# A two-layer gated cross-attention kernel: half of a normalised x transposed inside the attention's drain, and the operations of the middle in another order

## The chip, the cores and the metric

The kernel runs on one core of a Trainium2 chip. The metric is the time of one execution on the device in microseconds (us). TensorE (PE) multiplies and transposes, VectorE (DVE) and ScalarE (ACT) work element by element and empty the PSUM banks that TensorE fills, GpSimd (POOL) works element by element in SBUF and issues the indirect DMAs, and SyncE (SP) issues the plain DMAs. Each engine takes its instructions in the order in which they are written, and they wait for each other by semaphores (`wait_ge`).

## The reference, cut to what matters

x is 8 blocks of 128 tokens by 512 features, and the context has the same shape. Four residual updates follow each other:

```
x = x + tanh(g_xattn[0]) * cross_attention(layernorm(x), ctx)      # 32 heads, 8 kv heads
x = x + tanh(g_ffn[0])   * permuted_ffn(layernorm(x))              # t[:, perm], 16 small ffns, gelu, t[:, unperm]
x = x + tanh(g_xattn[1]) * group_attention(layernorm(x), ctx, ctx)
x = x + tanh(g_ffn[1])   * experts(layernorm(x))                   # top-1 of 8 experts
```

The third one is what the middle of the kernel computes (q is the normalised x, k and v are the context):

```
t = Wt @ v;  p = Wp @ q;  g = Wg @ k                 # products over the 128 tokens of a block
att = sum over a group of (p * g)                    # 8 groups of 16 tokens
y = Wz @ (att * t), group by group                   # so y = att * z with z = (Wz Wt) @ v
yn = (y - mean(y)) * rsqrt(var(y) + eps), in a group # var(y) = att^2 * var(z)
out = yn * gn_w + gn_b + v                           # v is the context, the residual
```

## The kernel before, in words

**Attention.** 64 units (8 groups g of heads, 8 blocks b) run through a software pipeline. For each engine the function `run` is given a list of stages, each with the number of units that it runs ahead or behind, and calls them in the list's order in every step. A unit goes through the q projection (L835 to L837), the scores (L825), mask and maximum (L750, L753), exponentials (L576), the transposition of p (L852), the values (L876 to L878), and the output projection (L865 to L867), of which `accumulate` (L782) adds the result to x. The last steps, in which no q projection is left, are the drain. Some stages do something only there, when `after(u, b, g, last)` holds: four of eight z products (`z01`, `z2`, `z3`, L893, one product of 512 columns each, copied to `s.z` by ScalarE, L652), and the first half (blocks 0 to 3) of the second layer norm: seed, Newton step on GpSimd, normalisation (L712, L811), transposition on TensorE into four PSUM banks (`transpose_x`, L888), and copies to `s.xT2` (`copy_xT`, L646, L803). `transpose_x` stands in the list with an offset of -5, behind the last unit's values, and the z products 2 and 3 ahead of it. They use banks 0 and 1, as the transpositions of blocks 0 and 1 do.

**Feed-forward.** In `middle`, SyncE stores the transposed x in four pieces of two blocks (L998, 512 KB each). Ahead of the first it waits for the last output projection (L562). GpSimd gathers the permuted features back in four indirect DMAs for each half (L1113), TensorE multiplies by `up` (L1289), ScalarE applies gelu (L1061), and TensorE multiplies by `down` (L1299). This goes in 12 packs: four of 512 tokens for the first half, eight of 256 for the second. VectorE copies the results (L1176), GpSimd scatters them (L1094: four for blocks 0 to 3, four for 4 and 5, four for 6 and 7), and SyncE loads each third (L1002), which TensorE transposes back (`transpose_y`, L1249) and VectorE adds to x (L1184).

**Middle.** For each third of the blocks: statistics of x on VectorE (L101, L104), half the variance plus eps (`layernorm_var`, L117), a seed for rsqrt by logarithm and exponential on ScalarE (`seed3`, L1038, L1040), a Newton step on GpSimd (`rstd3`, four small operations, L75 to L81), the shift -mean*rstd on VectorE (`negated_shift`, L110), the normalisation on ScalarE (`normalise3`, L1046), the product with Wp (`p_product`, L1258), and the product with g summed along the row on VectorE (L1216). GpSimd scales the context (`scale_ctx`, L1088) and adds it to x in place (`add_ctx`, L1108), which waits until ScalarE has normalised the block. ScalarE centres z (L1078), eight operations, ahead of the seed for y's variance (L1080, L1082). Then comes a Newton step on GpSimd and `a_col` on VectorE (L1234).

**Experts.** VectorE forms x3 = z * a_col + x block by block (`update`, L1506) with its statistics (L1511), TensorE transposes it (`transpose_x3`, L1667), the gate (L1673), logits (L1680), ranks and tile list follow, GpSimd scatters the rows to their experts (L1480), and 15 tiles of 128 rows go through the chosen experts' weights (L1744 to L1751).

The order around the change is written out by hand, in the lists of `run` and in the code of `middle` and `experts`.

## Time and profile before

| | us |
|---|---|
| median of 3 runs | 802.3 |
| lowest, highest | 801.92, 802.57 |
| profiled execution | 801.22 |
| its span | 799.4 |
| TensorE busy in the span | 748.2 |
| ScalarE, VectorE, GpSimd busy | 484.5, 469.5, 310.4 |

The mean granted clock of TensorE is 0.974 of full speed. The profiled execution's own time is longer than its span, since the span runs from the first to the last instruction. A share of busy time is a mean over stages: from 160 to 560 us TensorE is busy in every slice, and in the last fifth of the span its share falls to 0.6 to 0.9 in places. The lines L.. are those of the kernel before. "Idle before <-" names what ended the idle time of an engine.

### The profile page before, as it was taken

The page shows a single profiled execution, that of the slowest core. Times are in us where ns is not written, and L with a number is a line of the kernel's source. Part 1 is how long each engine was busy: PE and PEld are TensorE (multiplying, and loading weights), DVE is VectorE, ACT ScalarE, POOL GpSimd, SP SyncE. Part 2 cuts the span into 40 slices and gives each one's busy share as a digit, 9 for nine tenths or more (in the row PEclk, how much of TensorE's full clock was granted, in tenths as well). Part 3 has the DMA queues.
Part 4 walks back from the last instruction along what each step waited for, and adds up shares of the span by engine and source line. Part 5 has one row for each costly group of instructions (what it writes and reads, how often), then busy time and mean ns, then how long its engine had stood idle before and what let it go on. Part 6 is the DMA issues. An engine that isn't in the chain of part 4 may idle for free.

```text
span 799.4 us, 13560 instructions
## 1 busy us (share of the span) xinstructions
PE 748.2 (94%) x3925; PEld 604.0 (76%) x3925; DVE 469.5 (59%) x891; ACT 484.5 (61%) x1817; POOL 310.4 (39%) x623
## 2 busy tenths in 40 slices
PE   5999987999999999999999999999999979767997
PEld 3788876888888887888888788888887633336775
DVE  4786404565656565656565556565657645887652
ACT  4543336767676766676767566667665547456831
POOL 0331015353443453444354335354422336624242
PEclk9999999999999999999999999999999989966999
DMA  8545451302303303032132230330430065834232
GB/s 302 178 133 172 131 188 67 120 24 110 134 14 120 127 21 119 17 115 82 62 119 74 71 119 13 118 132 13 129 105 2 1 192 182 325 144 141 88 106 79
DMA packets 42125, 87.76 MB, mean 110 GB/s; under 512 B 5561, under 2 KB 26041, under 8 KB 38226
## 3 DMA queue, kind: packets, MB, share of 16 engines
q1 hardware_dynamic: 38884, 78.71, 29.1%
q0 software_dynamic: 3184, 8.41, 3.0%
q8 instruction: 21, 0.34, 0.2%
q14 instruction: 36, 0.29, 0.1%
HBM read 70.28 MB, written 35.57 MB: 132 GB/s over the span
## 4 chain that ended last, share of the span: by engine, by line
PE 71%; DVE 5%; ACT 4%; issue 2%; DMA 1%; POOL 1%; POOLq 0%; ACTq 0%; SPq 0%; DVEq 0%
PE banks L865 7%; PE banks L867 7%; PE banks L866 7%; PE banks L837 7%; PE banks L835 7%; PE banks L836 7%; PE banks L825 6%; PE banks L844 4%; PE banks L852 3%; PE banks L1750 2%; PE banks L1751 2%; PE banks L1749 2%; PE banks L876 2%; PE banks L878 2%; PE banks L877 2%
## 5 line engine op out<-in xcount | busy, mean ns | idle before, releaser
L576 ACT ACTIVATE p_sb<-p_sb,nmax 128x128 f32<-128x128 f32 x256 | 99.8, 391 | 132.2 <-DVE nmax L753 132.2
L674 POOL TENSOR_TENSOR v_lo<-v_raw,v_hi 128x128 fp32r<-128x128 f32 x64 | 29.6, 462 | 255.1 <-ACT v_hi L614 255.1
L776 DVE TENSOR_TENSOR pT_lo<-banks,pT_hi 128x512 fp32r<-128x512 f32 x64 | 44.2, 691 | 49.8 <-ACT pT_hi L589 49.8
L825 PEld LDWEIGHTS banks<-kT,qT_sb 128*128 128x128 f32 x512 | 67.0, 192 | 6.7 <-ACT qT_sb L584 1.8
L825 PE MATMUL banks<-kT,qT_sb 128*128 128x128 f32 x512 | 67.9, 276 | 1.4 <-ACT qT_sb L584 1.4
L679 POOL TENSOR_TENSOR p_sb<-p_sb,rsum 128x512 f32<-128x512 f32 x64 | 66.6, 1041 | 5.5 <-DVE rsum L772 5.5
L621 ACT ACTIVATE q_junk<-banks 128x128 f32<-128x128 f32 x256 | 66.1, 273 | 1.8 <-PE banks L837 1.8
L744 DVE TENSOR_TENSOR oT_lo<-banks,oT_hi 128x512 fp32r<-128x512 f32 x64 | 44.1, 689 | 35.6 <-ACT oT_hi L571 35.5
L398 PE MATMUL banks<-w_hi,ctx_hi 128*128 128x512 f32 x128 | 53.6, 419 | 9.3 <-DVE ctx_lo L329 9.3
L782 DVE SCALAR_TENSOR_TENSOR x_sb<-banks,tgates,x_sb 128x512 f32<-128x512 f32 x64 | 48.1, 751 | 15.2 <-PE banks L867 13.7
L571 ACT ACTIVATE oT_hi<-banks 128x512 fp32r<-128x512 f32 x64 | 38.0, 594 | 31.2 <-PE banks L878 27.0
L760 DVE TENSOR_SCALAR q_val<-q_ss 128x4 f32<-128x4 f32 x64 | 31.9, 498 | 41.3 <-ACT q_junk L621 41.3
L772 DVE RECIPROCAL rsum<-prob_sum 128x4 f32<-128x4 f32 x64 | 11.4, 178 | 72.2 <-ACT p_sb L576 72.2
L835 PE MATMUL banks<-w_hi,xT_hi 128*128 128x512 f32 x128 | 53.2, 416 | 0.0
L865 PE MATMUL banks<-odd_hi,oT_hi 128*128 128x512 f32 x128 | 52.9, 414 | 0.3 <-DVE oT_lo L744 0.2
L621 ACT ACTIVATION_READ_ACCUMULATOR q_junk<-banks 128x1 f32 x256 | 53.0, 207 | 0.0
L865 PE MATMUL banks<-w_hi,oT_hi 128*128 128x512 f32 x128 | 52.8, 412 | 0.0
L835 PE MATMUL banks<-odd_hi,xT_hi 128*128 128x512 f32 x128 | 52.6, 411 | 0.0
L400 PE MATMUL banks<-w_lo,ctx_hi 128*128 128x512 f32 x128 | 51.0, 398 | 0.0
L399 PE MATMUL banks<-w_hi,ctx_lo 128*128 128x512 f32 x128 | 50.7, 396 | 0.0
L837 PE MATMUL banks<-w_lo,xT_hi 128*128 128x512 f32 x128 | 50.6, 395 | 0.0
L836 PE MATMUL banks<-w_hi,xT_lo 128*128 128x512 f32 x128 | 50.5, 394 | 0.0
(271 smaller groups left out, 2099.7 us busy)
## 6 DMA issues: line engine op xcount, KB each, us to landing
sorted_x<-in_empty SPq DMA_DIRECT2D x8, 2064.0 KB, 9.1
w_raw<-in_wq_l SPq DMA_DIRECT2D x8, 1024.0 KB, 5.3
w_raw<-in_wo_l SPq DMA_DIRECT2D x8, 1024.0 KB, 4.8
exp_w<-in_exp_w_l SPq DMA_DIRECT2D x8, 1024.0 KB, 8.4
kT_scr<-kT_st SPq DMA_DIRECT2D x16, 256.0 KB, 2.3
v_scr<-v_st SPq DMA_DIRECT2D x16, 256.0 KB, 2.3
xs<-sorted_x SPq DMA_DIRECT2D x15, 258.0 KB, 2.8
v_raw<-v_scr SPq DMA_DIRECT2D x14, 256.0 KB, 2.6
```

Of the source, the lines that this page charges most:

```text
L398: pe.matmul(kv_ps[i % 3][:, :], ctx_hi[:, kt, tok], hi, start=(kt == 0), stop=False)
L400: last = pe.matmul(kv_ps[i % 3][:, :], ctx_hi[:, kt, tok], lo, start=False, stop=(kt == KT - 1))
L576: last = act.activation(p_sb[:, b % 2, h * P:(h + 1) * P], p_sb[:, b % 2, h * P:(h + 1) * P], ACT.Exp, bias=nmax[:, b % 2, h:h + 1], accum ...
L621: last = act.activation(junk[:, h * P:(h + 1) * P], q_ps[b % 2][:, h * P:(h + 1) * P], ACT.Square, accum_out=ss[:, b % 2, h:h + 1])
L679: pool.tensor_tensor(blocks(p_sb[:, b % 2, :]), blocks(p_sb[:, b % 2, :]), per_block(rsum[:, b % 2, :], P), ALU.mult).then_inc(p_done, 1)
L825: last = pe.matmul(s_ps[:, h * P:(h + 1) * P], qT_sb[:, b % 2, h * P:(h + 1) * P], kT[:, b * P:(b + 1) * P], start=True, stop=True)
L835: pe.matmul(q_ps[b % 2][:, :], xh, wq_hi[odd][:, kt, :], start=(kt == 0), stop=False)
L836: pe.matmul(q_ps[b % 2][:, :], xl, wq_hi[odd][:, kt, :], start=False, stop=False)
L837: last = pe.matmul(q_ps[b % 2][:, :], xh, wq_lo[odd][:, kt, :], start=False, stop=(kt == KT - 1))
L865: pe.matmul(o_ps[b % 2][:, :], oh, wo_hi[odd][:, h, :], start=(h == 0), stop=False)
L866: pe.matmul(o_ps[b % 2][:, :], ol, wo_hi[odd][:, h, :], start=False, stop=False)
L867: last = pe.matmul(o_ps[b % 2][:, :], oh, wo_lo[odd][:, h, :], start=False, stop=(h == HG - 1))
```

## The change

It has these parts:

- In the drain, `transpose_x` moves from behind the last values to ahead of the values of unit 62. The normalisation on VectorE moves ahead of `p_recip`. ScalarE copies three of four blocks, VectorE one. The z products 2 and 3 move behind the transpositions and wait for the copies of banks 0 and 1. The copies of z 2 and 3 stand at ScalarE's end. SyncE's wait for the last output projection is left out, and the stores wait for the copies by the new counts.
- GpSimd scales the context between its gathers and first scatters. `add_ctx` writes into the scaled context's own tile, so it no longer waits for the normalisation; x3 is formed from that tile, and the transposed x3 moves to where x was.
- The shift of the third layer norm is computed on GpSimd from a negated mean. The seeds read the variance itself. The first product of p and g stands ahead of the updates of blocks 6 and 7. ScalarE centres z in three groups. The variance of y is computed by a shorter way, its Newton step on VectorE.
- In the experts part, TensorE multiplies 128 columns of g by the unit matrix, nine times ahead of x3's first transposition and twice after each. Nothing reads the results: they go to a bank that the logits overwrite later.

```diff
             sp.dma_start(s.ctx_nat[:, :, :], d.ctx).then_inc(s.ctx_nat_ld, 16)
-            sp.wait_ge(o_done, UNITS)
...
-            run(act, [(oT_split, -2), (exps, 0), (copy_z01, 0), (qT_copy, 1), (pT_split, -1), (copy_z2, -1), (copy_z3, -1),
-                      (v_split, 2), (q_stats, 2), (seed_ln2, -3), (copy_xT, -6), (split_bias, 0)]
+            run(act, [(oT_split, -2), (exps, 0), (copy_z01, 0), (qT_copy, 1), (pT_split, -1), (copy_xT, -4), (copy_z23, -2),
+                      (v_split, 2), (q_stats, 2), (seed_ln2, -3), (split_bias, 0)]
...
-            run(dve, [(oT_split, -2), (mask_max, 0), (q_scale, 1), (p_recip, 0), (pT_split, -1), (q_half, 2),
-                      (copy_xT, -6), (normalise_ln2, -5), (accumulate, -2), (x_stats, -2), (split_bias, 0)])
+            run(dve, [(oT_split, -2), (mask_max, 0), (normalise_ln2, -4), (q_scale, 1), (p_recip, 0), (pT_split, -1), (q_half, 2),
+                      (accumulate, -2), (copy_xT, -4), (x_stats, -2), (split_bias, 0)])
...
             def z2(u, b, g, odd):
-                if after(u, b, g, B - 2):
-                    pe.wait_ge(s.z_copied[1], 1)
+                if after(u, b, g, B - 1):
+                    pe.wait_ge(xT_copied[1], 1)
                     z_product(2)
 
             def z3(u, b, g, odd):
                 if after(u, b, g, B - 1):
-                    pe.wait_ge(q_scaled, UNITS)
+                    pe.wait_ge(xT_copied[1], 2)
                     z_product(3)
...
-            run(pe, [(scores, 0), (q_proj, 2), (z01, 0), (q_transpose, 1), (p_transpose, -1), (z3, -1), (o_proj, -2),
-                     (z2, -1), (values, -1), (transpose_x, -5)])
+            run(pe, [(scores, 0), (q_proj, 2), (z01, 0), (q_transpose, 1), (p_transpose, -1), (z2, -1), (o_proj, -2),
+                     (transpose_x, -4), (values, -1), (z3, -1)])
...
                     if c == 0:
-                        sp.wait_ge(xT_copied[1 - pair], 2)
+                        sp.wait_ge(xT_copied[1], 2 + pair)
+                        reached(sp, xT_copied[0], pair)
...
             def seed3(c):
                 cols = slice(*THIRDS[c])
-                act.wait_ge(xval3_done, c + 1)
-                act.activation(xtmp[:, cols], xval[:, cols], ACT.Ln, scale=2.0).then_inc(xln3_ln, 1)
+                act.wait_ge(mv_done, THIRDS[c][1])
+                reached(act, xrstd3_done, c)
+                act.activation(xln3[:, cols], mv[:, cols, 1], ACT.Ln, bias=s.eps[:, 0:1]).then_inc(xln3_ln, 1)
...
             seed3(0)
             copy_g(5)
             copy_g(6)
             normalise3(0)
+            seed3(1)
+            centre(0, 1)
+            normalise3(1)
             copy_g(7)
-            seed3(1)
-            normalise3(1)
             seed3(2)
+            centre(2)
             normalise3(2)
-            act.wait_ge(col_step, 3)
-            for b in range(B):
-
-                act.activation(s.z[:, b, :], s.z[:, b, :], ACT.Identity, bias=s.nmean[:, b:b + 1]).then_inc(centred, 1)
-            act.wait_ge(yval_done, 1)
-            act.activation(yln[:, :], yval[:, :], ACT.Ln, scale=2.0).then_inc(yln_done, 1)
+            centre(3, 4, 5, 6, 7)
+            act.wait_ge(att_step, 2)
+            act.activation(yln[:, :], yvar[:, :], ACT.Ln, bias=s.eps[:, 0:1]).then_inc(yln_done, 1)
...
+                pool.wait_ge(xrstd3_done, c + 1)
+                pool.wait_ge(negm_done, c + 1)
+                pool.tensor_tensor(xshift[:, cols], negm[:, cols], xrstd[:, cols], ALU.mult).then_inc(xshift3_done, 1)
+
+            def add_ctx(*bs):
                 for b in bs:
                     pool.wait_ge(ctx_scaled, b + 1)
-                    pool.wait_ge(xln3_done, b + 1)
-                    pool.tensor_tensor(s.x[:, b, :], s.x[:, b, :], ctx_res[:, b, :], ALU.add).then_inc(res_done, 1)
+                    pool.wait_ge(x_done, b + 1)
+                    pool.tensor_tensor(ctx_res[:, b, :], s.x[:, b, :], ctx_res[:, b, :], ALU.add).then_inc(res_done, 1)
...
             def update_x(b):
-                if b == HB:
-                    shift(0)
                 dve.wait_ge(y_done, b + 1)
...
             updates_with_stats(dve, s, update_x, x_done, bn_done, mv_done, xval3_done, THIRDS[1:2])
+            negate_mean(1)
+            product(0)
             updates_with_stats(dve, s, update_x, x_done, bn_done, mv_done, xval3_done, THIRDS[2:3])
-            shift(1)
...
                 last.then_inc(x3T_done, 1)
+                keep_warm(2)
+
+            def keep_warm(n):
+                for i in range(n):
+                    pe.matmul(logit_ps[1][:, 0:P], s.ident[:, :], s.g[:, 0, 0:P], start=True, stop=True)
...
             pe.wait_ge(s.row_done, B)
+            keep_warm(9)
             for b in range(HB):
                 transpose_x3(b)
...
-            s.x3T = [beside(f"x3T{c}", [P, KT, HALF], 8 * c) for c in range(2)]
+            s.x3T = [s.at(f"x3T{c}", [P, KT, HALF], 8 * c) for c in range(2)]

```

TensorE in the drain, before: from the end of output projection 61, with z product 2 (L893), the values of unit 62 (L876 to L878), p's last transposition (L852) and z product 3.

```order
L893 MATMUL banks<-ctx_nat,mT 128x512 [waits z_copied1]
L876 MATMUL banks<-pT_hi,v_hi 128x512 [waits xT1_hi_done,kvw_lo_done,xrstd1_done]
L877 MATMUL banks<-pT_hi,v_lo 128x512
L878 MATMUL banks<-pT_lo,v_hi 128x512
L852 MATMUL banks<-ident_sb,p_sb 128x128 [waits xrstd1_done,xval1_done]
L852 MATMUL banks<-ident_sb,p_sb 128x128 x3
L893 MATMUL banks<-ctx_nat,mT 128x512 [waits kv_free]
```

The same place in the changed kernel, from its third transposition of x on (`hid` is the normalised x, L884 the transpositions, L871 the values, L847 p's, L889 the z product). Semaphores can bear the name of an earlier owner.

```order
L884 MATMUL banks<-ident_sb,hid 128x128 [waits xln2_done1]
L884 MATMUL banks<-ident_sb,hid 128x128 x3
L871 MATMUL banks<-pT_hi,v_hi 128x512 [waits xT1_hi_done,kvw_lo_done,xrstd1_done]
L872 MATMUL banks<-pT_hi,v_lo 128x512
L873 MATMUL banks<-pT_lo,v_hi 128x512
L847 MATMUL banks<-ident_sb,p_sb 128x128 [waits xrstd1_done,xval1_done]
L847 MATMUL banks<-ident_sb,p_sb 128x128 x3
L889 MATMUL banks<-ctx_nat,mT 128x512 [waits xT2_copied1]
```

The 16 transpositions of x took z product 2's place; z product 2 took z product 3's; and z product 3 went behind the last values, where the transpositions were.

GpSimd in the middle, before: from the last eight scatters (L1094) to its first additions.

```order
L1094 DMA yT_scr<-xg,perm_col 512x256 [waits yT_copied] x8
L1088 TENSOR_SCALAR ctx_res<-ctx_nat,tgates,tb 128x512 x2
L75 TENSOR_TENSOR xtmp<-xseed 128x4 [waits xseed3_done]
L77 TENSOR_TENSOR xtmp<-xtmp,xval 128x4 [waits newton3]
L79 TENSOR_TENSOR xtmp<-three_halves,xtmp 128x4 [waits newton3]
L81 TENSOR_TENSOR xrstd<-xseed,xtmp 128x4 [waits newton3]
L1088 TENSOR_SCALAR ctx_res<-ctx_nat,tgates,tb 128x512 x4
L1108 TENSOR_TENSOR x_sb<-x_sb,ctx_res 128x512 [waits xln3_done,ctx_scaled] x2
```

The same stretch in the changed kernel.

```order
L1098 DMA yT_scr<-xg,perm_col 512x256 [waits yT_copied] x8
L1116 TENSOR_TENSOR ctx_res<-x_sb,ctx_res 128x512 [waits x2_done,ctx_scaled] x2
L75 TENSOR_TENSOR xtmp<-xseed 128x4 [waits xval3_done,xseed3_done]
L77 TENSOR_TENSOR xtmp<-xtmp,xval 128x4 [waits newton3]
L79 TENSOR_TENSOR xtmp<-three_halves,xtmp 128x4 [waits newton3]
L81 TENSOR_TENSOR xrstd<-xseed,xtmp 128x4 [waits newton3]
L1110 TENSOR_TENSOR xshift<-neg_mean,xrstd 128x4 [waits neg_mean3_done,xrstd3_done]
L1116 TENSOR_TENSOR ctx_res<-x_sb,ctx_res 128x512 [waits x2_done,ctx_scaled] x2
```

The scalings are gone from here: two now stand between the two halves' gathers, and the other six between those gathers and the scatters of the first third. Additions stand ahead of each Newton step, and the shift behind it.

## Rows read from the trace of the kernel before

**Rows 1.** Chain of waits, 641 to 656 us: start us, us, what
```profile
642.52 0.39 SPq L998
...
642.96 4.07 DMA xT_scr<-xT
...
647.31 1.19 POOL xg L1113
```

**Rows 2.** Timeline, TensorE, drain to y's transpositions: start us, us, instruction [idle before <-releaser]
```profile
630.18 1.02 PE L893 MATMUL banks<-ctx_nat,mT 128*128 128x512 f32 x2
631.52 0.50 PE L876 MATMUL banks<-pT_hi,v_hi 128*128 128x512 f32 x1 [0.33 <-DVE pT_lo L776]
...
637.45 1.91 PE L888 MATMUL banks<-ident_sb,hid 128*128 128x128 f32 x16
639.29 0.50 PE L865 MATMUL banks<-odd_hi,oT_hi 128*128 128x512 f32 x1
...
652.26 1.62 PE L1289 MATMUL banks<-xg,up 32*128 32x512 f32 x8 [4.06 <-DMA xg<-xT_scr,perm_col]
...
663.60 0.71 PE L1289 MATMUL banks<-xg,up 32*128 32x256 f32 x8
...
677.92 2.17 PE L1249 MATMUL banks<-ident_sb,xT 128*128 128x128 f32 x16
```

**Rows 3.** Windows of 5 us: busy us of each engine, granted clock, DMA share, GB/s
```profile
655.00:660.00 5.00, 5.00 (x24) 1.19 (x20) 1.03 (x2) 2.77 (x3) 3.06 (x4) 0.54 0.66 175
710.00:715.00 5.00, 4.11 (x32) 2.68 (x31) 4.96 (x13) 3.27 (x7) 1.15 (x4) 0.92 0.00 0
715.00:720.00 5.00, 3.68 (x21) 1.69 (x19) 4.19 (x17) 1.63 (x5) 0.00 (x0) 0.76 0.00 0
```

**Rows 4.** Timeline, ScalarE, the middle
```profile
699.74 5.00 ACT L1078 ACTIVATE z<-z,nmean 128x512 f32<-128x512 f32 x8
704.64 0.19 ACT L1080 ACTIVATE yln<-yval 128x8 f32<-128x8 f32 x1
```

**Rows 5.** Timeline, VectorE, small operations of the middle
```profile
644.77 0.16 DVE L75 TENSOR_TENSOR xtmp<-xseed 128x4 f32<-128x4 f32 x1 [0.38 <-ACT xseed L1020]
...
688.91 1.32 DVE L117 TENSOR_SCALAR xval<-mv 128x2 f32<-128x2 f32 x1
...
697.08 1.20 DVE L110 SCALAR_TENSOR_TENSOR xshift<-mv,xrstd 128x2 f32<-128x2 f32 x1 [1.79 <-POOL xrstd L81]
...
706.22 0.17 DVE L1234 TENSOR_TENSOR a_col<-att,yrstd 128x8 f32<-128x8 f32 x1 [2.29 <-POOL yrstd L81]
```

**Rows 6.** Timeline, TensorE, the gate's products
```profile
711.96 1.07 PE L1673 MATMUL banks<-x3T,gate_c 128*32 128x512 f32 x8 [0.69 <-ACT x3T L1421]
...
717.39 1.74 PE L1673 MATMUL banks<-x3T,gate_c 128*32 128x512 f32 x8 [0.69 <-ACT x3T L1421]
```

**Rows 7.** Chain of waits, a unit of attention
```profile
584.96 0.89 PE banks L825 x8
```

**Rows 8.** Timeline, GpSimd, drain to the middle
```profile
625.60 4.15 POOL L712 TENSOR_SCALAR hid<-x_sb,mv,xrstd 128x512 f32<-128x512 f32 x2
...
654.28 0.94 POOL L1113 DMA_INDIRECT xg<-xT_scr,perm_col  x1 [2.02 <-DMA xT_scr<-xT]
...
668.14 1.52 POOL L1088 TENSOR_SCALAR ctx_res<-ctx_nat,tgates,tb 128x512 f32<-128x512 f32 x2
...
678.80 0.97 POOL L1094 DMA_INDIRECT yT_scr<-xg,perm_col  x1 [0.30 <-issue]
...
688.93 2.51 POOL L1108 TENSOR_TENSOR x_sb<-x_sb,ctx_res 128x512 f32<-128x512 f32 x2
```

**Rows 9.** DMA issues, 625 to 745 us: out<-in, queue, count, KB each, median us to landing
```profile
xT<-yT_scr SPq DMA_DIRECT2D x1, 1024.0 KB, 5.5
...
yT_scr<-xg,perm_col POOLq DMA_INDIRECT x12, 2.7
```

**Rows 10.** DMA issues, 654 to 659.5 us, the second half's gathers
```profile
xg<-xT_scr,perm_col POOLq DMA_INDIRECT x4, 3.9
```

116 lines of the change are left out of this document (64 added, 52 removed).

## The prediction

> **What bounds the kernel now.** I read the chain of waits first, then TensorE's timeline from the last attention units on, then the windows, and GpSimd's, ScalarE's and VectorE's timelines beside them. Up to 620 us TensorE is full and the change leaves its order alone there. From 642 us nothing is full: the chain goes through a store, a gather, chains of small operations, and TensorE runs partly at half clock. The whole change lies in 620 to 730 us, so the sum is made on that stretch; the tiles of the experts behind it (a full TensorE) only shift. The profiled execution took 801.22 us, span 799.4 and 1.8 around it; the median shown is 802.3, 1.1 above it.
>
> Four things fix the length of the stretch. (1) The store of the first half of xT, 4.07 us, starts at 642.96, after the last output projection, and the first gather of GpSimd follows it; TensorE stands still for 4.06 us until 652.26 [rows 1, 2]. (2) Its clock is then at 0.54 of full on average from 655 to 660, that is 1.2 GHz for nearly all of it [rows 3]. (3) In the middle, the coefficient a_col is ready at 706.22 + 0.17 = 706.39, behind eight centrings of z on ScalarE (5.00 us), a logarithm at 704.64, and a Newton step on GpSimd for which VectorE waits 2.29 us [rows 4, 5]. (4) From there to the tiles VectorE and TensorE alternate, and TensorE's clock comes and goes: the gate's eight instructions take 1.07 us at 711.96 and 1.74 at 717.39 [rows 6].
>
> **Drain of the attention.** After output projection 61, TensorE had z product 2 (from 630.18) and a wait, and came to unit 62's values at 631.52. Now the 16 transpositions, 1.91 us with the tail of the last (1.84 from start to start, 639.29 less 637.45), stand there: values at 632.0, 0.5 late [rows 2]. The other end: the second normalisation of GpSimd (4.15 us for two, ended at 629.75 [rows 8]) and VectorE's two, now ahead of its reciprocal, may collide, which I bound at one more of GpSimd's, 2.1 us late. Behind them wait values, the last transposition of p and the projection. Later the 16 transpositions are gone from 637.45, and a z product (0.9, from 1.02 us for one with its tail) stands there instead. Yet the last projection starts when VectorE has split oT, 639.29 before, and VectorE's row is the same there: I take 0.3 late, between 0 and 2. The three copies of xT on ScalarE, under 0.6 us each like its centrings, stand ahead of unit 62's oT and end by 632.5, before those values are done at 632.9. **Term A: +0.3.**
>
> A second cost stands at 644.7. GpSimd now scales two blocks of the context (0.76 each [rows 8]) just when VectorE runs its Newton step at 644.77 [rows 5]. In these rows a small VectorE operation takes 1.32 us (a tensor_scalar of 128x2) or 1.20 (a product of two SBUF inputs) while GpSimd adds blocks, against 0.16 for the Newton step's without it [rows 5]. So one or two of the five small operations can stand behind a block: 0 to 1.5 us, I take 0.4, as the blocks are short. **Term B: +0.4.** The Trainium skill, SBUF — State Buffer, § Who interferes with whom, has the rule: the port pair that VectorE and GpSimd share is a lock, so the later one waits for the whole instruction of the other; two SBUF inputs or a two-port mode take it. The two rows agree. By it this change, which puts GpSimd's blocks beside VectorE's statistics, has a price of its own: it is the last rival below.
>
> **Feed-forward.** SyncE no longer waits for the last projection: the first pair of blocks is stored at about 632.3 and the second at 633, landed by 637.5 with 4.07 us a store [rows 1]; four gathers, 1.25 us apart and landed 3.9 us after their start [rows 10], are done by 646. TensorE then starts the first pack as soon as the second half's copies are done. They ended at 648.8 on ScalarE and 649.4 on VectorE, so it starts at 649.7 instead of 652.26: 2.55 us. Its idle time shrinks from 4.06 to under 1.5, so I take the full clock for the first packs. Pack 4 started 11.3 us after pack 0, 663.60 less 652.26 [rows 2]. At full clock a pack of 512 columns takes 2.4 to 2.5 us, by which pack 4 comes 8.8 us after pack 0 with the first gelu waiting for the table load: 2.5 us. **Term C: −5.1** (−2.6 if the clock drops all the same, or if the second half's gathers, at 654.28 [rows 8], stay where they are: these must land by 658.5, 3.9 us from their start [rows 10], and start at 653 to 653.7 now that the second store has the transfers to itself).
>
> GpSimd gives some of that back. Its order is now: gathers until 658.0; two scalings 1.5; four times a scatter (0.97 and 0.3 between) and a scaling 0.76, the fourth scatter starting at 665.6; landed 2.7 later; load of yU 5.5: 673.9 [rows 8, 9]. Before, the transpositions of y started at 677.92 [rows 2]. So TensorE waits for that load and not for the feed-forward (which ends at 671): I gain 3.9, not 5.1. The eight scatters behind end at 678.4, were 679.77, and the last load, half as large, lands by 684.2, for a transposition due at 684.9: no wait. **Term D: +1.2** (0 to +3).
>
> **Middle, from y to a_col.** Per step:
> - The shift for x3's normalisation moves from VectorE to GpSimd. For VectorE it was a wait before block 4, and 1.20 us behind an addition for the last group. One small operation, 0.2 us as GpSimd's others, and a hand-over replace it; the seed reads the variance itself, so the half variance (1.32 us beside GpSimd's additions [rows 5]) leaves ScalarE's chain.
> - ScalarE's order becomes seed 1, centre 0 and 1, normalise, seed 2, centre 2, normalise, centre 3 to 7. Three centrings (1.9 us) now lie in waits for GpSimd. The last normalisation ended just ahead of the centrings at 699.74 [rows 4]; by the new order, reckoned with the 3.9, it ends at 693.4.
> - Five centrings (5 x 0.62) end at 696.5, when the variance of y is ready too (last product 695.3, sum over groups 0.6, two small operations). Logarithm and exponential 0.45, Newton on VectorE four times 0.2, a_col 0.2: 698.0.
> Against 706.39 that is 8.35, of which 3.9 are counted: **Term E: −4.4** (−2.5 to −6). The additions of the context, 1.25 us each [rows 8], lose their wait for the normalisation, and end by 694.4, ahead of the 698.
>
> **Unread products.** Nine stand after the sum over groups, two after each of eight transpositions, 25 in all, 128 columns each: 0.22 us at full clock (0.89 for eight instructions, four products), some 0.45 at half [rows 7]. The first nine take 2.0 to 4.0 us in TensorE's wait for a_col and x3, which is about 3 now; a pair and a transposition take 0.9 (1.7 cold) against VectorE's 1.27 a block, so they hold nothing up once the clock is full. Before, the clock was back at full for most of 710 to 715 (mean 0.92), behind x3's first transpositions, and lower again in 715 to 720 (0.76) [rows 3]. Kept full through the ranks and logits (the gate 0.67 less [rows 6], the logits and two groups of rank products, each of a like length, some 0.6 to 0.9), both the tile list and the scatters would come 2 us sooner: the second comes through GpSimd's scatters, which follow each other. The products stop at the last transposition, though, so I take part: **Term F: −1.4** (+0.9, if cold products delay x3, to −2.2). The Trainium skill, TensorE: Matmul & The Clock Gate, § What's actually happening, says the throttled clock is the default and activity releases it, with which the rise at 710 agrees.
>
> Sum: 0.3 + 0.4 − 5.1 + 1.2 − 4.4 − 1.4 = −9.0. So 801.22 − 9.0 = 792.2 for a profiled execution, and 802.3 − 9.0 = **793.3** as the median.
>
> **Rivals.**
> - *More passes through.* GpSimd's queue is not the bound (loads land sooner, D = 0), the clock holds to the tiles (F = −2.2), B = 0: −11.4, 790.9. For it: the landings are medians of few [rows 9]. Against: twelve scatters at 1.27 apart are a fixed queue. Chance 0.2.
> - *The early store is hidden.* The second half's gathers or GpSimd's longer queue bound the feed-forward, so C and D together give 1.0 and not 3.9: −6.1, 796.2. For it: pack 4 needs the gather from the second store, whose start moves only by 1. Against: the gathers that started at 654.28 had landed 5 us ahead of pack 4 at 663.60. Chance 0.2.
> - *Unread products are in the way.* The clock is at half when they start and x3's transpositions fall behind VectorE: F = +0.9 instead of −1.4, and 0.7 of E lost: −6.0, 796.3. Chance 0.07.
> - *Slower: VectorE stands behind GpSimd.* Seven operations at 644 to 646 (Newton, shift, two normalisations) behind a scaling of 0.76, and ten in the middle (three half variances, three negated means, four on the deviations of z) behind an addition of 1.25: 5.3 + 12.5 = 17.8 us if each waits a whole one. With 0.4 already counted: −9.0 + 17.4 = +8.4, 810.7. It decides from about half of them (9.4 us) on. For it: 1.32 and 1.20 [rows 5]. Against: GpSimd's blocks fill only parts of that time, and the half variance is no longer what ScalarE waits for. Chance 0.04. This is what the rule of the page SBUF — State Buffer in the Trainium skill, § Who interferes with whom, would do here.
>
> My forecast has 0.49. What this measurement can tell from no change is 0.2%, 1.6 us. All cases but the last and a corner of the two partial ones are faster: 0.93, same 0.02, slower 0.05. Range: from 789.5 (the first rival with E at −5.8) to 797.2 (the partial ones with A at 1.3), leaving out the slow one and the tails.
>
> **What would show it.** SyncE's first store near 632 and the first gather near 637.5; TensorE's first up product near 650 with a granted clock of 1.00 behind it; y's transpositions near 674 behind a load; a_col near 698; a clock of 1.00 from there to the last x3 transposition; the tiles starting near 731. It would be wrong if pack 4 or the y transpositions don't move, if small VectorE operations of over 1 us stand ahead of xrstd or a_col, or if the last projection is over 2 us late.

## The result, and the profile after

The changed kernel took 796.38 us (median of four executions, 795.69 to 799.69); the kernel before took 802.11 us in the same comparison. The ratio is 0.9946, 95% interval 0.9929 to 0.9964: 0.5% faster, where 1.1% was forecast. The sign and the range were right. The size was not: by the ratio half of the forecast gain was missing, by the medians (5.7 us gained of 9.0) a good third. Timed again beside the experiments, the changed kernel took 796.18 us (six executions, 794.83 to 799.52), ratio 0.9935, interval 0.9914 to 0.9956. Ratios here and below leave out three slow executions: one of 1089 us of the kernel before, and one each (865 and 856 us) of two of the later kernels.

There are two profiles of it. The first fell on the slowest of its four executions (799.69 us). The second (span 793.5 us, clock 0.988) is nearer to the median, and the rows below are from it where nothing else is said. This table cuts the spans at the same points of the program, in us:

| from one point to the next | before | changed, first profile | changed, second profile |
|---|---|---|---|
| start to the eight z products | 642.16 | 642.51 | 641.89 |
| to the first pack of the feed-forward | 10.10 | 7.54 | 7.55 |
| to the first g products (feed-forward done) | 23.84 | 21.25 | 21.24 |
| to y's first transpositions | 1.82 | 5.96 | 4.90 |
| to y's transpositions of blocks 4, 5 | 6.66 | 10.73 | 8.08 |
| to the first p product | 3.28 | 3.29 | 3.28 |
| to the end of a_col | 18.53 | 13.72 | 13.72 |
| to the split of the experts' weights (ew_lo) | 23.39 | 22.22 | 22.21 |
| to the first tile | 12.34 | 12.95 | 12.34 |
| to the end of the span | 57.28 | 57.63 | 58.29 |

In the fourteen profiles of this study the z products started between 640.3 and 644.4, though the code ahead of them is of two kinds only: where an execution stands at that point says little of the edit. So positions are counted from there. From the end of output projection 61 to the z products, however, the drain takes the same time in every execution of one order: 11.96 to 12.00 us in the three profiles with the drain of before (642.16 less 630.18 is 11.98), 12.38 to 12.40 in the eleven with the changed drain (641.89 less 629.50 is 12.39).

TensorE's timeline answers to [rows 2, 6]. The 16 transpositions stand at 629.50, ahead of the values. The first pack comes 7.55 behind the z products, and the fifth (658.17) 8.73 us after it, not 11.34. Behind the g products the engine has nothing for 2.91 us, and then y's 16 transpositions take 3.32 us instead of 2.17. The gate's two groups take 1.06 and 1.07 us (1.07 and 1.74 before).

```profile
629.50 1.91 PE L884 MATMUL banks<-ident_sb,hid 128*128 128x128 f32 x16
631.16 0.48 PE L871 MATMUL banks<-pT_hi,v_hi 128*128 128x512 f32 x1
...
641.89 3.59 PE L1251 MATMUL banks<-ctx_nat,mT 128*128 128x512 f32 x8
...
649.44 1.99 PE L1304 MATMUL banks<-xg,up 32*128 32x512 f32 x12 [0.73 <-DVE xT L1158]
...
658.17 0.71 PE L1304 MATMUL banks<-xg,up 32*128 32x256 f32 x8
...
670.68 1.98 PE L1255 MATMUL banks<-ctx_nat,wgT 128*128 128x512 f32 x4
675.58 3.32 PE L1261 MATMUL banks<-ident_sb,xT 128*128 128x128 f32 x16 [2.91 <-DMA xT<-yT_scr]
...
706.08 1.06 PE L1694 MATMUL banks<-x3T,gate_c 128*32 128x512 f32 x8 [0.24 <-ACT x3T L1436]
...
711.91 1.07 PE L1694 MATMUL banks<-x3T,gate_c 128*32 128x512 f32 x8 [0.24 <-ACT x3T L1436]
```

The windows answer to [rows 3], in the same columns. 655 to 660 is at 1.00 where it was 0.54; the new hole is in 675 to 680; 710 to 715 is at 1.00 where it was 0.92.

```profile
655.00:660.00 5.00, 4.79 (x40) 1.20 (x33) 3.34 (x8) 4.83 (x6) 4.05 (x6) 1.00 0.55 152
675.00:680.00 5.00, 4.42 (x26) 4.45 (x26) 3.52 (x7) 0.00 (x0) 3.98 (x5) 0.66 0.56 194
710.00:715.00 5.00, 4.06 (x35) 2.94 (x33) 4.22 (x20) 2.57 (x6) 0.60 (x3) 1.00 0.01 3
```

GpSimd's timeline [rows 8]: gathers of the first half from 636.09, the two scalings that stand beside VectorE's Newton step, the second half's gathers, two more scalings, the fourth scatter. The load of yU can be issued only when this has landed.

```profile
636.09 1.19 POOL L1125 DMA_INDIRECT xg<-xT_scr,perm_col  x1 [5.21 <-DMA xT_scr<-xT]
...
644.30 1.52 POOL L1092 TENSOR_SCALAR ctx_res<-ctx_nat,tgates,tb 128x512 f32<-128x512 f32 x2 [3.26 <-DVE tb L1167]
654.46 0.98 POOL L1125 DMA_INDIRECT xg<-xT_scr,perm_col  x1 [8.63 <-DMA xT_scr<-xT]
...
659.23 1.51 POOL L1092 TENSOR_SCALAR ctx_res<-ctx_nat,tgates,tb 128x512 f32<-128x512 f32 x2
...
666.93 1.03 POOL L1098 DMA_INDIRECT yT_scr<-xg,perm_col  x1 [0.17 <-issue]
```

VectorE, then ScalarE [rows 4, 5]: two of four Newton operations take 0.58 and 0.48 us where they took 0.16, the half variance is down from 1.32 to 0.73, a_col no longer waits for GpSimd, and five centrings are left ahead of the logarithm.

```profile
644.50 0.58 DVE L75 TENSOR_TENSOR xtmp<-xseed 128x4 f32<-128x4 f32 x1 [0.38 <-ACT xseed L1019]
...
645.36 0.48 DVE L79 TENSOR_TENSOR xtmp<-three_halves,xtmp 128x4 f32<-128x4 f32 x1
...
687.15 0.73 DVE L117 TENSOR_SCALAR xval<-mv 128x2 f32<-128x2 f32 x1
...
700.49 0.17 DVE L1246 TENSOR_TENSOR a_col<-att,yrstd 128x8 f32<-128x8 f32 x1
```

```profile
696.06 3.15 ACT L1067 ACTIVATE z<-z,nmean 128x512 f32<-128x512 f32 x5
699.13 0.28 ACT L1084 ACTIVATE yln<-yvar,eps 128x8 f32<-128x8 f32 x1
```

The first profile shows the same wait in a worse execution: here the fourth scatter needed 4.14 us to land and the load of yU 5.38 (chain of waits), and TensorE came back from 3.98 idle us at half clock for longer.

```profile
667.59 4.14 DMA yT_scr<-xg,perm_col
...
671.75 5.38 DMA xT<-yT_scr
```

```profile
677.26 3.65 PE L1261 MATMUL banks<-ident_sb,xT 128*128 128x128 f32 x16 [3.98 <-DMA xT<-yT_scr]
```

### The profile page after: what moved, and what is told of

Read it like the earlier page. It is cut to its first block, busy times and chain, and to the rows that moved or that the text cites. A ratio compares the mean times of both kernels' runs of the same rounds, so it can differ in the third digit from the quotient of the medians.

```text
span 797.8 us, 13672 instructions
## 1 busy us (share of the span) xinstructions
PE 751.3 (94%) x3975; PEld 610.2 (76%) x3975; DVE 468.2 (59%) x893; ACT 485.4 (61%) x1818; POOL 310.7 (39%) x622
## 4 chain that ended last, share of the span: by engine, by line
PE 70%; DVE 6%; ACT 4%; issue 2%; DMA 1%; POOL 1%; POOLq 0%; ACTq 0%; DVEq 0%
PE banks L860 7%; PE banks L862 7%; PE banks L861 7%; PE banks L832 7%; PE banks L831 7%; PE banks L830 7%; PE banks L820 6%; PE banks L839 4%; PE banks L847 3%; PE banks L1771 2%; PE banks L1772 2%; PE banks L1773 2%; PE banks L873 2%; PE banks L871 2%; PE banks L872 2%
```

## The experiments

My theory after the two profiles was this: the early store gives what was forecast, but the change also puts six scalings of the context between GpSimd's gathers and scatters (five of them ahead of the fourth scatter, one behind it). The first third of y is then scattered late, loaded late, and TensorE waits for it (3 to 4 us) and loses its full clock in the wait (1.4 to 4 us more). Rivals were that the transfers are late whatever GpSimd does, and that the clock has another cause. Each kernel ran 4 to 12 times beside the kernel before, in three groups, in which the kernel before took 801.5, 802.6 and 801.8 us. A profile shows one execution, and since the starts of the z products scatter over 4 us, medians that differ by 1 or 2 us do not tell two kernels apart here; their intervals then overlap.

**The scalings behind the last scatter.** Against the changed kernel:

```diff
-            scale_ctx(range(2, 4))
             for jt in range(KT):
                 scatter(0, jt)
-                scale_ctx(range(4 + jt, 5 + jt))
...
             for jt in range(KT):
                 scatter(2, jt)
+            scale_ctx(range(2, B))
             add_ctx(0, 1)
```

> GpSimd's six scalings of the context leave the place between the gathers and the first third's scatters and stand behind the last scatter. Theory (GpSimd's queue held y's load up): the fourth scatter starts at 663.7 to 664.5 instead of 667.59, the load of yU is issued by 668, y's transpositions start at 673.3 right behind the two g products instead of 677.26, the clock stays at 1.00: 4.0 us in fast executions, up to 7.4 in one like that profiled. Less up to 1 us, since 4.6 us of scalings now lie ahead of the additions and of the first reciprocal root. Time 791.5 to 793.5. Rival 1 (the load waits for the transfers, not for the queue: the fourth scatter took 4.1 us to land instead of 2.7): the scatters start sooner but land as late, y at 676 or later, time within 1 us of the changed kernel. Rival 2 (what binds is the middle behind, VectorE's and ScalarE's chain): y starts sooner but a_col moves by under 1 us, 795.5 to 796.5.

Measured: 794.59 us, ratio 0.9907 (0.9887 to 0.9928), 1.6 below the changed kernel in the same group (the intervals overlap), where 791.5 to 793.5 was expected. The wait went exactly as the theory said: fourth scatter at 663.96, y's transpositions at 673.09 directly behind the g products, at full clock (GpSimd, then TensorE).

```profile
663.96 0.97 POOL L1098 DMA_INDIRECT yT_scr<-xg,perm_col  x1 [0.30 <-DVE xg L1183]
...
676.04 4.52 POOL L1092 TENSOR_SCALAR ctx_res<-ctx_nat,tgates,tb 128x512 f32<-128x512 f32 x6
```

```profile
673.09 2.16 PE L1260 MATMUL banks<-ident_sb,xT 128*128 128x128 f32 x16
...
679.73 1.04 PE L1260 MATMUL banks<-ident_sb,xT 128*128 128x128 f32 x8
...
685.41 2.07 PE L1269 MATMUL banks<-xln,wpT 128*128 128x512 f32 x2 [3.79 <-ACT xln L1046]
```

y's blocks 4 and 5 are 4.5 us sooner than in the second profile of the changed kernel, counted from the z products (37.27 against 41.77). But 3.1 us of it were lost again behind: 2.4 up to the first p product (5.68 us instead of 3.28) and 0.7 from there to a_col (14.42 instead of 13.72). Six scalings (4.52 us) and two additions (2.47) now stand ahead of GpSimd's part of the reciprocal root. Beside them VectorE's half variance, an operation on 128x4 elements that took 0.17 us before, took 3.83 us and ended with the second addition (683.0); the chain of waits goes through it, and GpSimd's Newton step starts 0.17 us behind it.

```profile
679.21 3.83 DVE L117 TENSOR_SCALAR xval<-mv 128x4 f32<-128x4 f32 x1
```

TensorE waits 3.79 us for the normalised x, and the first p product runs at half clock (2.07 instead of 1.12). I had allowed up to 1 us for all that. So the cause was found, and the edit was a poor cure.

**The wait filled with unread products.**

```diff
             for b in range(2):
                 g_product(b)
+            for i in range(16):
+                pe.matmul(s.ps[4][:, 0:P], s.ident[:, :], s.ctx_nat[:, 0, 0:P], start=True, stop=True)
```

> Sixteen unread products of 128 columns stand in TensorE's wait between the first two g products and y's transpositions (from 673.3 on, 0.22 us each at full clock, 3.5 us). Theory (the idle time costs the clock, and this about 3.4 us of the profiled execution, nothing in the fast ones): y's transpositions still start at 677.0 to 677.5, take 2.0 to 2.2 us instead of 3.65, granted clock 1.00 in 680 to 685; all runs at 795.5 to 796.5, none near 800. Rival (the low clock has nothing to do with the wait, but with what load comes before): clock as low as before, spread as before, 795.7 to 800.

Measured: 796.23 us, the changed kernel's time, single runs from 793.5 to 797.6, wider than expected, though none is near 800. The profile shows the mechanism (x32 is 16 products, two rows each):

```profile
671.12 3.73 PE L1322 MATMUL banks<-ctx_nat,ident_sb 128*128 128x128 f32 x32
674.76 2.19 PE L1261 MATMUL banks<-ident_sb,xT 128*128 128x128 f32 x16
...
681.81 1.09 PE L1261 MATMUL banks<-ident_sb,xT 128*128 128x128 f32 x8 [0.21 <-DMA xT<-yT_scr]
```

With products in the wait, y's 16 transpositions take 2.19 us, and the window 675 to 680 is at 1.00. In every profile of this study the rows agree: after 2.91, 3.98 or 4.95 idle us there, these transpositions took 3.32, 3.65 and 3.65 us; after none, or 0.94 or 1.06, they took 2.16 to 2.19. So the idle time costs the clock. It didn't pay here, because 16 products (3.73 us) outlast a wait of 2.9: 0.4 us was left in the profile, and nothing in the medians. The Trainium skill, TensorE: Matmul & The Clock Gate, § What's actually happening, calls the throttled clock the default, which activity releases; the trace agrees.

**The changed kernel again.**

> The changed kernel once more, for its spread: its four runs so far were 795.7, 795.7, 797.0 and 799.7 us, and the profiled one was the slowest of them (TensorE idle for 3.98 us before y's transpositions, then 5 us at half clock, these transpositions 3.65 us instead of 2.17). Theory (GpSimd's queue holds y's load up, and the clock falls in that wait in some executions only): a median near 796.2, single runs between 795.5 and 800, and a profile with either the idle time and a clock near 1.00 in 680 to 685, or the idle time and 0.50 there. Rival (the idle time comes in every execution and with it the low clock; the spread has another source): 0.50 to 0.60 in 675 to 685 in this profile too, whatever its time.

Measured: 796.18 us, and 2.91 idle us with a clock of 0.66 in 675 to 680 but 1.00 in 680 to 685, where the first profile had 0.59 and 0.50. Both forms that I had named occur mixed: the wait comes in each profile, and how long the clock stays down behind it varies. Between the two profiles the stretch from the g products to y's blocks 4 and 5 differs by 3.7 us of the 4.3 by which the spans differ.

**The scalings where GpSimd waits anyway.**

```diff
                     pool.wait_ge(col_step, 2)
-                    scale_ctx(range(2))
+                    pool.wait_ge(zmv_done, 1)
+                    scale_ctx(range(5))
...
-            scale_ctx(range(2, 4))
...
-                scale_ctx(range(4 + jt, 5 + jt))
...
+            scale_ctx(range(5, B))
             add_ctx(0, 1)
```

> Five of the eight scalings stand where GpSimd waits for the second store anyway, released when VectorE has done z's first statistics (651.2), until 655.1; the other three behind the last scatter. None is left at 644.9 beside VectorE's Newton step, and none between gathers and scatters. Theory: as with the scatters first (y at 673, -4.0), and in addition the Newton step's 0.58 and 0.48 go back to 0.16 and TensorE's second transpositions start 0.7 us sooner (646.6 instead of 647.36), the first pack at 649.3: -4.7 to -5.5 against the changed kernel's fast runs, 790.5 to 792. Rival (small operations of VectorE cost nothing on the path there, since the gelu's table load or the copies set the start of the packs): same time as with the scatters first.

Measured: 791.31 us, ratio 0.9868 (0.9844 to 0.9893), 4.9 below the changed kernel. Five scalings lie in the wait for the second store; TensorE's second transpositions are back at +4.07 behind the z products (+4.85 with scalings beside the Newton step), and y's wait is 1.06 us at full clock.

```profile
648.61 3.77 POOL L1092 TENSOR_SCALAR ctx_res<-ctx_nat,tgates,tb 128x512 f32<-128x512 f32 x5 [9.12 <-DVE zmv L1164]
652.53 0.99 POOL L1126 DMA_INDIRECT xg<-xT_scr,perm_col  x1
```

```profile
644.41 1.97 PE L1287 MATMUL banks<-ident_sb,hid 128*128 128x128 f32 x16 [0.48 <-DVE hid L1153]
...
671.40 2.19 PE L1261 MATMUL banks<-ident_sb,xT 128*128 128x128 f32 x16 [1.06 <-DMA xT<-yT_scr]
```

**Each part alone.** Next the parts were put into the kernel before, one at a time. First the drain: transpositions, copies, z products and stores as in the change; middle, GpSimd's order and x3 as before.

```diff
-            sp.wait_ge(o_done, UNITS)
...
-            run(pe, [(scores, 0), (q_proj, 2), (z01, 0), (q_transpose, 1), (p_transpose, -1), (z3, -1), (o_proj, -2),
-                     (z2, -1), (values, -1), (transpose_x, -5)])
+            run(pe, [(scores, 0), (q_proj, 2), (z01, 0), (q_transpose, 1), (p_transpose, -1), (z2, -1), (o_proj, -2),
+                     (transpose_x, -4), (values, -1), (z3, -1)])
```

> The kernel before with the part in the attention's drain alone: the first half's transpositions and stores early, the z products and copies moved for it; the middle, GpSimd's order and x3 are those of the kernel before, and no unread products. Theory (the early store is worth its full size, and the scalings between gathers and scatters, which the change adds at the same time, ate most of it): counted from the eight z products behind the last output projection, the first pack starts at +6.8 (before +10.1), the feed-forward ends at +28, the fourth scatter starts near +21.5, y's transpositions at +29.8 to +30.2 right behind the g products (before +35.8, changed kernel run again +33.7): 5.6 to 6 us faster than before, 795.5 to 796.5, which is what the whole change reaches. Rival (the load of yU is late whatever GpSimd does, since the second store lands late): y's transpositions at +32.5 to +34, 798.5 to 800.

Measured: 795.98 us against 802.63, ratio 0.9907 (0.9883 to 0.9931). This part alone is worth at least about what the whole change is worth (the intervals overlap). Its rows are the forecast's term C without the rest: first pack at +6.76, feed-forward done at +28.01, y at +29.89 with no wait. From a_col to ew_lo this kernel, which has no unread products, took 22.26 us, as the changed kernel with them did.

```profile
641.01 3.59 PE L1236 MATMUL banks<-ctx_nat,mT 128*128 128x512 f32 x8
...
669.02 1.98 PE L1240 MATMUL banks<-ctx_nat,wgT 128*128 128x512 f32 x4
670.90 2.19 PE L1246 MATMUL banks<-ident_sb,xT 128*128 128x128 f32 x16
```

Then the middle alone: GpSimd's order, the additions, the shift, the centrings, the Newton step, the seeds and the places of x3 of the change, with the drain of before and no unread products. The lines of the change that it keeps, in part:

```diff
+            centre(3, 4, 5, 6, 7)
...
+                pool.tensor_tensor(xshift[:, cols], negm[:, cols], xrstd[:, cols], ALU.mult).then_inc(xshift3_done, 1)
...
+            scale_ctx(range(2, 4))
             for jt in range(KT):
                 scatter(0, jt)
+                scale_ctx(range(4 + jt, 5 + jt))
```

> The kernel before with the middle's part alone (GpSimd's order of scalings and additions, the context added into its own tile, the shift on GpSimd, ScalarE's centrings in the waits, the last Newton step on VectorE, the seeds from the variance) and the attention's drain as before, no unread products. Theory: from the first p product to a_col 13.7 us instead of 18.5 (-4.8), the Newton step beside the scalings +0.8 as in the changed kernel, no wait before y's transpositions, because the feed-forward is late enough here: -4.0, 797 to 798. Rival (the middle's gain needs the early start, since the additions and scalings otherwise meet the statistics): 799 or more. Rival (the scalings hold up y's load here too): y's transpositions more than 1 us behind the g products, 799.

Measured: 799.05 us, ratio 0.9951 (0.9931 to 0.9972), a wide spread (795.8 to 803.4): a gain of 3.6 us by the medians, where 4.0 and a time of 797 to 798 were expected. The profile fell on the slowest of the twelve executions (803.42 us). The first p product to a_col took 13.73 us, as expected, and y's transpositions had no wait. The Newton step had no cost, against my expectation: the first gathers end later here, so the scalings start at 654.22, far behind it. Of the rivals, the time came to 799, but the cause named for it did not show: y had no wait. What the profile shows instead is that from a_col to ew_lo it took 26.25 us, not 23.39: 2.9 us are given back there, at a clock of 0.50 from 710 to 735.

**Without the unread products.** The changed kernel with both calls of `keep_warm` left out:

```diff
                 last.then_inc(x3T_done, 1)
-                keep_warm(2)
...
             pe.wait_ge(s.row_done, B)
-            keep_warm(9)
```

> The changed kernel without its 25 unread products. Theory: a_col is where it was, and from there to the split of the experts' weights (ew_lo) it takes 23.4 us as before instead of 22.2: 1.2 us slower than the changed kernel, 797.2 to 797.6. Rival (the products do nothing that lasts to the end, since the tiles wait for the scatters and loads): 796.0 to 796.5. Rival (they are in the way of x3's transpositions): 795 to 796.

Measured: 798.22 us, ratio 0.9961 (0.9932 to 0.9989), above the 797.2 to 797.6 expected. Seven of the twelve executions took 795.4 to 798.3 us, the other five 801.8 to 806.0, and the profile is from one of these (803.67). In it a_col (705.82) to ew_lo took 26.25 us again, and the windows show it:

```profile
705.00:710.00 5.00, 2.91 (x13) 1.96 (x14) 4.86 (x15) 1.47 (x3) 0.00 (x0) 0.72 1.01 424
710.00:715.00 5.00, 4.31 (x19) 2.25 (x20) 4.97 (x13) 2.20 (x6) 1.78 (x4) 0.50 0.13 54
715.00:720.00 5.00, 4.31 (x23) 3.63 (x25) 3.69 (x16) 2.34 (x5) 0.00 (x0) 0.50 0.00 0
```

TensorE is busy for 4.3 to 5.0 of each 5 us from 710 to 725 and stays at 0.50 all the same, that is 1.2 GHz, until 735. The kernel before had come back to 0.92 in 710 to 715 [rows 3]. With the middle's part in and the products out, that return came in none of three profiles (this one, the middle alone, and one below), with the middle of before and the products out in both (the kernel before and the drain alone, 1.00 in 710 to 715); why is left open. So the products are worth 4.0 us in the profiled stretch. In the medians it is about 2 us (798.22 against 796.2 to 796.4), and the intervals overlap.

**The unread products alone in the kernel before** (the two calls and the function, nothing else):

```diff
                 last.then_inc(x3T_done, 1)
+                keep_warm(2)
...
             pe.wait_ge(s.row_done, B)
+            keep_warm(9)
```

> The kernel before with the 25 unread products alone. Theory (the unread products hold the clock at 1.00 through x3's transpositions, and what they give depends on what the clock would do without them): the kernel before had 0.92 and 0.76 in 710 to 720, so only 1 to 1.4 us can be had here: from a_col to ew_lo 22.1 to 22.4 instead of 23.39, time 1.0 to 1.4 us below the kernel before. Rival (nothing at all, the nine products start at half clock behind the sum over groups and delay x3): 0 to +1.

Measured: 802.66 us against 801.75, ratio 1.0010 (0.9995 to 1.0024): nothing, or a trace slower, not the 1.0 to 1.4 us expected. That is the rival's size without its cause: x3's first transposition starts 0.85 us behind a_col, no later than before (0.93). From a_col to ew_lo the profile has 22.37 instead of 23.39, but the first tile follows 35.4 behind a_col where it was 35.7, and the feed-forward took 25.4 us in this execution instead of 23.8. In this kernel, where the clock was back at 0.92 without them, the products buy nothing that lasts.

**Scalings behind the first gathers too.** GpSimd computes the two scaled columns itself (VectorE did) and scales three blocks right behind its first gathers and VectorE's last split of oT (`oT_lo_done`), four in the wait for the second store, one behind the last scatter. The lines added for the first two:

```diff
+                    pool.tensor_tensor(s.tw[:, :], s.gn_w[:, :], s.tgates[:, 1:2], ALU.mult).then_inc(col_step, 1)
+                    pool.tensor_tensor(s.tb[:, :], s.gn_b[:, :], s.tgates[:, 1:2], ALU.mult).then_inc(col_step, 1)
                     pool.wait_ge(ctx_nat_ld, 16)
+                    pool.wait_ge(s.oT_lo_done, UNITS)
                     pool.wait_ge(col_step, 2)
-                    scale_ctx(range(2))
+                    scale_ctx(range(3))
+                    pool.wait_ge(zmv_done, 1)
+                    scale_ctx(range(3, 7))
```

> The kernel with the scalings in the wait for the second store, changed further: GpSimd computes the two scaled columns itself and scales three blocks right behind the first four gathers (641.7 to 644.2), four more when z's first statistics are done, one behind the last scatter. Theory (a GpSimd block costs VectorE something only where VectorE works from two SBUF inputs; here it stands beside the last accumulation, whose input is in PSUM, and bn_stats): second transpositions still at +4.1 counted from the eight z products, the second gathers as soon as the store has landed, y's transpositions up to 0.4 sooner, time 790.5 to 791.5 against 791.3 for the one before. Rival (any VectorE operation waits for a block): the last accumulation and statistics take 0.5 to 1.5 us longer, second transpositions at +4.8 to +5.5, time 792 to 793.

Measured: 790.81 us against 802.63, ratio 0.9847 (0.9824 to 0.9869). It is 1.5% below the kernel before, and not told apart from the previous version (791.31): the step itself shows no gain clear of noise. Three scalings (from 644.11 to 646.4) lie beside the last accumulation and its statistics, which take 0.75 and 0.69 us as they do without them, and the Newton step is at 0.16 again (VectorE, then GpSimd):

```profile
644.60 0.75 DVE L777 SCALAR_TENSOR_TENSOR x_sb<-banks,tgates,x_sb 128x512 f32<-128x512 f32 x1 [3.12 <-PE banks L862]
645.38 0.69 DVE L86 BATCH_NORM_STATS2 bn<-x_sb 128x6 f32<-128x512 f32 x1
...
647.01 0.16 DVE L75 TENSOR_TENSOR xtmp<-xseed 128x4 f32<-128x4 f32 x1 [0.51 <-ACT xseed L1019]
```

```profile
644.11 2.27 POOL L1092 TENSOR_SCALAR ctx_res<-ctx_nat,tgates,tb 128x512 f32<-128x512 f32 x3 [0.20 <-POOL tb L1121]
```

The Trainium skill, SBUF — State Buffer, § Who interferes with whom, says that a VectorE instruction with at most one SBUF input, outside its two-port modes, doesn't contend with GpSimd. The accumulation has one (its other input is in PSUM), the Newton step's products have two; the trace agrees on both sides.

**That kernel once more, without and with more unread products.** The first of the three is the same kernel, the second leaves out the two calls as above, the third has nine products more, by the diff behind the expectations.

> The best kernel so far (scalings right behind the first gathers and in the wait for the second store) once more, as the measure for the next two. Its median was 790.8, runs 789.7 to 793.8: 790.3 to 791.5.

> The same kernel without the 25 unread products. Theory: the clock stays at 0.50 from 5 us behind a_col to the tiles, as in the changed kernel without them (0.50 from 710 to 735), a_col to ew_lo 26.25 us instead of 22.2: 3 to 4 us slower than the kernel with them, 793.8 to 795. Where the profile of an execution shows the clock back at 1.00 behind x3's first transpositions, 22.5 to 24 us and 1 us slower. Rival (what the profile showed was one unlucky execution, the unread products are worth 1.2 us at most): 791.5 to 792.2.

> The same kernel with nine more unread products: three behind the first half's rank products and six behind the second half's logits, in TensorE's waits of 0.7 and 1.6 us. There the clock was 0.56 and 0.50 from 715 to 725, and the second half's rank and count products took 3.1 us (715.70 to 718.85). Theory: at full clock these take half, a_col to ew_lo 20.7 to 21.3 instead of 22.15: 1 to 1.5 us faster, 789.3 to 790. Rival (the clock falls all the same, and six cold products of 0.45 us end later than the wait of 1.6): 0 to 1 us slower, 790.8 to 791.8.

```diff
             ranks(0)
+            for i in range(3):
+                pe.matmul(x3T_ps[1][:, 0:P], s.ident[:, :], s.g[:, 0, 0:P], start=True, stop=True)
             logits(1)
+            for i in range(6):
+                pe.matmul(x3T_ps[1][:, 0:P], s.ident[:, :], s.g[:, 0, 0:P], start=True, stop=True)
             ranks(1)
```

Measured: 791.37 us again (ratio 0.9859, 0.9840 to 0.9878), 793.12 without (0.9884, 0.9868 to 0.9900), 791.37 with nine more (0.9872, 0.9857 to 0.9888). Without them the clock was 0.50 from 695 to 725 and a_col to ew_lo took 26.28 us. In the median that is 1.75 us, less than the 3 to 4 that I had expected, and the two intervals overlap. The two profiled executions are those of the medians: from the z products to the end they differ by 4.2 us (145.98 and 150.20), and their z products start 2.3 us apart the other way. How much of the 4.2 stays in a mean over many executions is open. With nine more, a_col to ew_lo fell from 22.80 to 21.04, as the theory said, and next to nothing came of it: a_col to the first tile went from 35.15 to 34.81. The time fell within the rival's range, but not by its cause. Without the nine the chain of waits goes over ew_lo and TensorE's 32 products behind it; with them it goes through the last of x3's scatters and the load of the first tile's rows (without the nine, then with them):

```profile
720.55 9.67 PE banks L1747 x32
```

```profile
722.76 3.89 DMA sorted_x<-xrow,pos_i
...
727.04 3.15 DMA xs<-sorted_x
```

So once ew_lo comes 1.2 us sooner or more, x3's eight scatters on GpSimd are the bound. Their first starts 15.24 us behind a_col here (15.23 without the nine), their last 25.28 (25.23). The second half's ranks come sooner (TensorE, 714.17), but then three scatters take 1.50 us and not one. TensorE of this kernel, then its last scatter, then that of the kernel without the nine:

```profile
712.40 1.58 PE L1739 MATMUL banks<-g_sb,ident_sb 128*128 128x128 f32 x12
714.17 0.41 PE L1726 MATMUL banks<-hot,rows_before 128*128 128x32 f32 x2 [0.19 <-DVE hot L1561]
```

```profile
722.76 1.51 POOL L1498 DMA_INDIRECT sorted_x<-xrow,pos_i  x1 [0.30 <-issue]
```

```profile
722.15 1.50 POOL L1498 DMA_INDIRECT sorted_x<-xrow,pos_i  x1 [0.31 <-issue]
```

## Why the prediction was wrong, step by step

- **The step that failed is term D**, "GpSimd gives some of that back", +1.2. It was +4.5: 3.08 us more from the g products to y's transpositions, and 1.42 more from there to blocks 4 and 5. I had named the right queue and all its pieces. First, the second half's gathers started at 654.46, not at 653 to 653.7. The copies ended when I had said; but I took 4.07 us for the store, the first half's price [rows 1], though the last store of the kernel before had a longer landing in the same trace. The rows are the DMA issues of before from 648.5 on, and the chain of waits of the changed kernel:

```profile
xT_scr<-xT SPq DMA_DIRECT2D x1, 512.0 KB, 5.1
```

```profile
649.39 4.80 DMA xT_scr<-xT
```

That put the queue 1.3 us back (fourth scatter at 666.93, not 665.6). Its landing (2.77) and the load (5.72) were near the 2.7 and 5.5 of [rows 9], so y came at 675.58 and not at 673.9. Second, I gave the wait its length but no price at the clock, although I had just priced the same thing for the wait before the first pack [rows 2, 3]. With the scalings moved away both parts are gone, although in the kernel with the scatters first the second half's gathers start no sooner (12.60 us behind the z products, 12.57 in the changed kernel): the late store alone holds nothing up.
- **The rival that came true in size** is "the early store is hidden": −6.1, 796.2, to which I gave 0.2. What C and D leave together is small (0.65 us with B in it), as it said. Of its two causes the second, GpSimd's longer queue, is the one. Only it doesn't bind the feed-forward, as the rival said, but y's transpositions behind it.
- **Term C, −5.1**, and **term B, +0.4**: together −5.15 (2.55 and 2.60 in the table) against −4.7. The first part is 3.3 when no scalings lie beside the Newton step (first pack at +6.77 instead of +10.10), so B is +0.78, which is what the rows say: 0.58 + 0.21 + 0.48 less three times 0.16 is 0.79. The second part is 2.6 against this one profile of the kernel before; in the two other profiles with the late store (the middle alone, the unread products alone) the feed-forward took 25.3 and 25.4 us and not 23.8, at half clock for longer, so against them it would be 4.1.
- **Term A, +0.3**: +0.41, from 11.98 to 12.39 us between output projection 61 and the z products, in both profiles. Right. The positions at that point (642.51 and 641.89, before 642.16) don't show it, since the executions start the drain at different times.
- **Term E, −4.4**: −4.81 in both profiles, 13.73 with the middle alone. Right (from 706.39 to 698.0 are 8.39 us, not the 8.35 of the working, which changes nothing). But in the profile of the middle alone 2.9 of it are given back, at half clock through x3.
- **Term F, −1.4**: −1.18 against the kernel before. The sum was near, and part of that is luck: the drain alone came to 22.26 us, 1.13 less than before, with no products at all. I compared with the clock that the kernel before had behind a_col; in none of the three profiles with the changed middle and no products did it come back. There the changed kernel lost 2.9 where with the products it won 1.2. Nor did the products hold the clock through the ranks and logits: in the second profile it fell to 0.69 and 0.50 in 715 to 725.
- **Not in the sum:** the 57.28 us from the first tile to the end were 57.63 and 58.29, and 57.2 to 58.5 in the other kernels: differences between executions.

In total, with the second profile: −0.27 (start) − 5.15 + 4.50 − 4.81 − 1.18 + 1.01 (tiles) = −5.9, the difference of the spans 799.4 and 793.5. The first of these is +0.41 of term A and −0.68 by which this execution came sooner to the drain. The forecast was −9.0. D missed it by 3.3, the tiles by 1.0, F by 0.2 and A by 0.1; B with C, and E were better by 0.9 together, and the sooner start gave 0.7; 3.1 in all. Of the signs that I had named, the first gather came at 636.09 (forecast 637.5), the first pack at 649.44 (650), y at 675.58 (674), a_col at 700.66 (698) and the first tile at 735.21 (731). Of the other rivals, "more passes through" needed a queue that is no bound (D = 0): that is what the kernels with moved scalings showed, 791.3 and 790.8, near its 790.9, but they are other kernels. "Unread products are in the way" didn't come: x3's first transposition starts 0.84 us behind a_col, before 0.93. "VectorE stands behind GpSimd" didn't come in the changed kernel: small operations beside blocks were longer by 0.2 to 0.6 us each, never by a whole block. It did come for one operation of the kernel with the scatters first, by 3.7 us beside scalings and additions that follow each other without a gap.

## What to carry to other kernels

Work that fills an idle engine is free only if nothing behind it in the same queue releases someone else: put it into the wait itself (here ahead of the gathers), not between the end of the wait and the transfers that follow, and not where VectorE's small operations on the chain would stand beside it. Price a new wait of TensorE twice, by its length and by the half clock behind it. Measure the parts of a change apart: here the drain's alone was worth about the whole, and the others took from it and from each other.

## What was not expected of the hardware

- In the changed kernel without unread products TensorE stayed at the granted clock 0.50 for 25 us (710 to 735), in the first 15 of which it was busy for 4.3 to 5.0 of each 5 us with x3's transpositions, the gate, logits and ranks. With the 25 products that nobody reads it was at 1.00 until 715, through all of x3's transpositions, and they held nothing up: a transposition of x3 and its pair lie within VectorE's pace.
- A scatter of x3 takes GpSimd 0.97 to 1.04 us, but 1.49 to 1.51 when VectorE has begun to split the experts' weights some time before: the last three with nine more products (the split starts at 718.52, these scatters at 719.17, 720.96 and 722.76), the last one in the kernel without the nine. There is no simple order in it: in ten profiles a scatter that started 1.07 to 1.16 us behind the split took 0.97 to 1.05 us, the one 0.65 us behind it here took 1.49. That an earlier split lengthens the queue that the tiles wait for is read from the traces, not tested.
- The same DMA pattern lands at different times from execution to execution: the fourth scatter of y's first third took 2.77, 4.14 and 4.65 us in three profiles with the same order around it. TensorE's wait behind it was 2.91, 3.98 and 4.95 us long, and the way from the g products to y's blocks 4 and 5 took 12.98, 16.69 and 17.44 us. Executions of the changed kernel differ by up to 4.9 us; this is one part of it.
- One VectorE operation on 128x4 elements took 3.83 us, not 0.17, while GpSimd worked off scalings and additions of 128x512 one behind the other, and ended with the last of them. Beside two scalings alone, products of this size took 0.58, 0.21 and 0.48 us.
